# A cross-attention, state-space and feed-forward layer on one core: two carry schedules, a shared buffer across a phase boundary, and the last two blocks of the quantised feed-forward

## The reference, cut to what matters

```
c   = mean over heads of top-32 attention(x, ctx) @ V                # attention stage
x1  = layernorm(x)*(1 + film) + film                                  # modulate
y   = s4d(x1)                     # K = 2 Re sum_n C' exp(dt A l), causal convolution over 256 tokens
xt  = x + y*(1 + film) + film;  xt += gelu(layernorm(xt)@W1+b1)@W2+b2;  x2 = x + layernorm(xt)
# quantised feed-forward, on layernorm(x2)
xq  = round(x*127/max|x|) per token;  wq = ternary weights
h   = silu(depthwise_conv3(xq @ w1q) + b)
out = x2 + (round(h*127/max|h|) @ w2q) * (max|h|/127) * mean|w2|
```

## Time and profile before

| | us |
|---|---|
| three runs | 4005.41, 4005.66, 4013.56 |
| median | 4005.66 |
| profiled execution: its time | 4004.6 |
| its span | 4002.8 |
| busy in the span: PE, DVE, ACT, POOL | 3197.8, 2965.5, 2268.3, 1585.6 |
| s4d, by its first and last instructions | about 2027 to 2551 |
| feed_forward | about 2551 to 3547.9 |
| bit_feed_forward | 3547.9 to the end |

### The profile page before, as it was taken

The page is one execution under the profiler, slowest core; times in us unless marked ns, Lnnn a source line. Parts: engine busy times, 40 slices in busy tenths (PEclk is TensorE's granted clock), DMA queues, the critical chain, the costliest instruction groups (busy, mean ns, idle before and its releaser), DMA issues. The chain is left out here.

```text
span 4002.8 us, 54326 instructions
## 1 busy us (share of the span) xinstructions
PE 3197.8 (80%) x17201; PEld 2126.4 (53%) x17201; DVE 2965.5 (74%) x7375; ACT 2268.3 (57%) x2924; POOL 1585.6 (40%) x1268
## 2 busy tenths in 40 slices
PE   7547758887776787777977777589999999948998
PEld 3224334444443344445755555377777777736775
DVE  7789999999999999984569987434444443469897
ACT  4478779898985898971123333133323322337876
POOL 0025556555664555665300010013333232217775
PEclk9858878888887788878999998799999999979999
DMA  8700000000000000002213343633444443440212
GB/s 310 265 33 10 10 8 10 12 10 10 10 13 7 10 10 10 10 5 101 83 48 81 87 95 84 178 120 124 131 129 129 132 127 83 122 101 15 67 49 65
DMA packets 263201, 290.53 MB, mean 73 GB/s; under 512 B 53805, under 2 KB 176319, under 8 KB 261893
## 3 DMA queue, kind: packets, MB, share of 16 engines
q1 hardware_dynamic: 241112, 254.05, 21.2%
q10 hardware_dynamic: 18764, 18.34, 1.6%
q0 software_dynamic: 3040, 14.94, 1.0%
HBM read 218.82 MB, written 68.45 MB: 72 GB/s over the span
## 5 line engine op out<-in xcount | busy, mean ns | idle before, releaser
L1103 PE MATMUL up<-ctx,attnT 128*128 128x384 f32 (+1 forms) x1664 | 706.8, 580 | 45.0 <-ACT attnT L973 45.0
L1075 PE MATMUL score<-KT,q 64*128 64x512 f32 (+1 forms) x1792 | 385.5, 524 | 346.3 <-ACT S L933 243.5
L830 DVE MAX8 cand<-S 128x8 f32<-128x146 f32 (+1 forms) x2816 | 601.3, 295 | 53.7 <-ACT S L933 34.6
L789 POOL TENSOR_TENSOR S<-S 128x512 f32<-128x512 f32 (+1 forms) x224 | 424.7, 1929 | 354.9 <-DVE S L835 354.9
L1103 PEld LDWEIGHTS up<-ctx,attnT 128*128 128x128 f32 (+1 forms) x1664 | 361.6, 228 | 314.7 <-issue 149.8
L835 DVE SCALAR_TENSOR_TENSOR S<-S,tops,E 128x3202 f32<-128x3202 f32 x128 | 472.8, 3757 | 14.6 <-ACT E L964 14.6
L1075 PEld LDWEIGHTS score<-KT,q 64*128 64x128 f32 x1792 | 174.3, 237 | 547.2 <-ACT S L933 397.9
L933 ACT ACTIVATE S<-score 128x1024 f32<-128x1024 f32 (+1 forms) x448 | 402.9, 931 | 87.8 <-PE score L1075 87.0
L2179 DVE TENSOR_TENSOR ff_gelu<-ff_whole,ff_gelu 128x512 fp32r<-128x512 f32 x128 | 97.3, 761 | 427.2 <-ACT ff_gelu L2373 427.2
L942 ACT ACTIVATE E<-S,below 128x3202 bf16<-128x3202 f32 x128 | 379.6, 2966 | 40.3 <-DVE below L870 19.4
L964 ACT ACTIVATE E<-S,ebias 128x3202 f32<-128x3202 f32 x128 | 376.4, 2965 | 23.8 <-DVE S L835 13.4
(11 more groups left out here) (422 smaller groups left out, 5976.6 us busy)
## 6 DMA issues: line engine op xcount, KB each, us to landing
s_hankel<-scratch_K SPq DMA_DIRECT2D x128, 256.0 KB, 4.5
ff_w_low<-scratch_w1l SPq DMA_DIRECT2D x112, 256.0 KB, 2.7
ff_w_low<-scratch_w2l SPq DMA_DIRECT2D x112, 256.0 KB, 2.8
xt_prep<-in_x SPq DMA_DIRECT2D x8, 1024.0 KB, 8.7
scratch_xt<-xt_prep SPq DMA_DIRECT2D x8, 1024.0 KB, 8.2
next_prep<-in_ffn_w_t POOLq DMA_DIRECT2D x8, 1024.0 KB, 11.4
q<-scratch_qt SPq DMA_DIRECT2D x128, 64.0 KB, 1.9
mod_xt<-in_x_turned SPq DMA_DIRECT2D x32, 256.0 KB, 2.6
```

The source lines that it names most:

```text
L789: nc.gpsimd.tensor_tensor(S[:, b, 0, chunk(j)], S[:, b, 0, chunk(j)], S[:, b, 1, chunk(j)], ALU.add).then_inc(s["summed01"], 1)
L830: nc.vector.max(cand[:, h, 8 * k:8 * k + 8], S[:, b, h, k * SEG:min((k + 1) * SEG, G)])
L1075: last = nc.tensor.matmul(score[bank(p, j)][:, e, 0:w], lhsT=q[at, b, part, h // 2, :], rhs=KT[at, h // 2, chunk(j)], start=(part == 0), s ...
L1103: last = nc.tensor.matmul(up[:, 0:DV], lhsT=attnT[0:w, e, c - 4 * g, :], rhs=ctx[0:w, c, :], start=(c == 0), stop=(c == GC - 1))
```

## The change

In s4d a carry takes `first` (a part) and `halves` (one part or two). The first pair and the last pair are carried in two single steps of half the width; table(3) comes ahead of the first carry; `S_ready` counts parts. `chunk_turn(0)` comes ahead of `kernel_weights(1)` on POOL.

Between the feed-forwards: two tensors, `wide` and `lead`, outlive both. In feed_forward they hold y, u, q, qT, h and the film and bias rows; in bit_feed_forward `wide` holds the rounded hidden rows `gq`, `lead` the q and steps of a block and the ones. At the end of feed_forward SP loads block 0's q and steps into `lead` and two quarters of W1 into `wide`. The last group's stores count on a semaphore that is awaited in bit_feed_forward only (load(7), and the first writes to `gq`). The last steps are turned by PE into four rows of 128, copied by ACT and stored from there.

At the end of bit_feed_forward ACT rounds six j of block 7 and DVE two (`quantise_late`); PE takes blocks 7 and 8 piece by piece, j outside and k inside, each j when it is rounded, into eight different banks; block 8's x2 rows go to the free `conv` and are loaded ahead.

```diff
@@ s4d, POOL
-                        pool.wait_ge(s["S_ready"], G)
+                        pool.wait_ge(s["S_ready"], 2 * G)
-                for g in range(PARTS):
-                    if g:
-                        kernel_weights(g)
-                    if g % 2:
+                chunk_turn(0)
+                for g in range(1, PARTS):
+                    kernel_weights(g)
+                    if g % 2 and g > 1:
                         chunk_turn(g // 2)
@@ s4d, DVE
-                def carry(G):
+                def carry(first, halves):
...
+                    width = GP * halves
+                    at = slice(GP * (first % 2), GP * (first % 2) + width)
...
-                    dve.wait_ge(s["U_copied"], UG * 2 * (G + 1))
+                    dve.wait_ge(s["U_copied"], UG * (first + halves))
...
-                    add(2).then_inc(s["S_ready"], 1)
+                    add(2).then_inc(s["S_ready"], halves)
...
-                for G in range(PARTS // 2 - 1):
+                table(2)
+                table(3)
+                carry(0, 1)
+                carry(1, 1)
+                for G in range(1, PARTS // 2 - 1):
                     table(2 * G + 2)
-                    carry(G)
+                    carry(2 * G, 2)
                     table(2 * G + 3)
-                carry(PARTS // 2 - 1)
-                dve.wait_ge(s["S_ready"], PARTS // 2)
+                carry(PARTS - 2, 1)
+                carry(PARTS - 1, 1)
+                dve.wait_ge(s["S_ready"], PARTS)
@@ s4d, PE
-                    pe.wait_ge(s["S_ready"], g // 2 + 1)
+                    pe.wait_ge(s["S_ready"], g + 1)
@@ feed_forward, SP, ahead of store_x(QUADS - 1)
+                sp.wait_ge(s["qT_stored"], 16 * (QUADS + 1))
+                sp.wait_ge(s["rowstep_stored"], 16 * (QUADS + 1))
+                sp.wait_ge(s["modulated"], QUAD * QUADS)
+                sp.wait_ge(s["film_read"], QUAD * QUADS)
+                sp.wait_ge(s["biased"], QUADS)
+                lead_q, lead_step = lead_of(both)
+                sp.dma_start(lead_q, dram["qT"][:, :, MARGIN - 1:MARGIN + BIT_STEP + 1]).then_inc(passed_on["lead_in"], 16)
+                sp.dma_start(lead_step, dram["rowstep"][0:BIT_STEP + 2].partition_broadcast(P)).then_inc(passed_on["lead_in"], 16)
+                for k in range(2):
+                    sp.dma_start(early_w1_of(both, k), dram["w1q"][:, :, k * BANK:(k + 1) * BANK]).then_inc(passed_on[f"w1_in{k}"], 16)
@@ feed_forward, ACT
-                    if k == 0:
+                    if k == 0 and g < QUADS - 1:
...
+                act.wait_ge(s["rowstep_turned"], 1)
+                nc.scalar.activation(step_row, fp[0][0:QUAD, 0:P], ACT.Copy).then_inc(s["rowstep_row"], 1)
                 for k in range(QUAD):
                     copy_q(QUADS - 1, k)
-                act.wait_ge(s["qT_stored"], 16 * (QUADS + 3))
-                act.wait_ge(s["rowstep_stored"], 16 * (QUADS + 2))
+                act.wait_ge(s["rowstep_row"], 1)
+                act.dma_start(dram["rowstep"][QUAD * P * (QUADS - 1) + 1:QUAD * P * QUADS + 1].rearrange("(k p) -> k p", p=P), step_row).then_inc(passed_on["last_q_stored"], 16)
+                act.wait_ge(s["qT_stored"], 16 * (QUADS + 1))
+                act.wait_ge(s["rowstep_stored"], 16 * (QUADS + 1))
@@ feed_forward, PE
+                pe.wait_ge(s["gelu_done"], FC * QUADS)
+                pe.wait_ge(s["rowstep_ready"], QUADS)
+                nc.tensor.transpose(fp[0][0:QUAD, 0:P], rowstep[:, (QUADS - 1) % 2], const["ident"][:]).then_inc(s["rowstep_turned"], 1)
@@ bit_feed_forward
-    BY_ACT = [5] * (BLOCKS - 2) + [JC, 3]
+    BY_ACT = [5] * (BLOCKS - 2) + [6, 3]
...
+        gq = both["wide"][:].bitcast(BF16).rearrange("p (b f t) -> p b f t", b=2, f=FC)
...
-        out_at[BLOCKS - 2][2:] = hp[0][:, 0, :], hp[0][:, 1, :]
-        out_at[BLOCKS - 1][:2] = hp[1][:, 0, :], hp[1][:, 1, :]
+        out_at[BLOCKS - 2] = [hp[k // 2][:, k % 2, :] for k in range(QUAD)]
+        out_at[BLOCKS - 1] = [op[0], op[1], mp.rearrange("p k t -> p (k t)"), step_rows]
@@ bit_feed_forward, SP
-                load(0)
-                for k in range(HID // BANK):
+                sp.dma_start(taps[:], a["conv_w_cols"]).then_inc(s["taps_in"], 16)
+                sp.dma_start(tap_bias[:], a["conv_b_cols"]).then_inc(s["taps_in"], 16)
+                for k in range(2, HID // BANK):
...
+                    if m == BLOCKS:
+                        sp.wait_ge(s["raised"], ALL)
+                        for k in range(QUAD):
+                            sp.dma_start(last_x2[0:rows(BLOCKS - 1), k], dram["x2"][rows_at(BLOCKS - 1, k), :]).then_inc(s["last_x_in"], 16)
@@ bit_feed_forward, POOL
                     pool.wait_ge(s["scaled"], JC * n + j + 1)
+                    if n == 0 and j == BY_ACT[n]:
+                        pool.wait_ge(passed_on["last_q_stored"], LAST_Q)
@@ bit_feed_forward, DVE
+                def quantise_late(n):
+                    dve.wait_ge(passed_on["last_q_stored"], LAST_Q)
+                    for j in range(BY_ACT[n], JC):
+                        dve.wait_ge(s["scaled"], JC * n + j + 1)
+                        v.tensor_scalar(gq[:, n % 2, 2 * j:2 * j + 2, 0:QUAD * rows(n)], part(n, j), ROUND, ROUND, ALU.add, ALU.subtract).then_inc(s["late_quantised"], 1)
...
+                    if i == ALL + STEPS_AT - JC:
+                        quantise_late(BLOCKS - 2)
                     if i == ALL - JC + SCALE_AT:
                         quantise_last(BLOCKS - 1)
@@ bit_feed_forward, PE
+                def pieces(n, order, begin, end):
+                    r = rows(n)
+                    for j in order:
+                        if j < BY_ACT[n]:
+                            pe.wait_ge(s["rounded"], by_act(n) + j + 1)
+                        else:
+                            pe.wait_ge(s["late_quantised"], by_pool(n) - by_pool(BLOCKS - 2) + j - BY_ACT[n] + 1)
+                        for k in range(QUAD):
+                            for f in (2 * j, 2 * j + 1):
+                                last = nc.tensor.matmul(out_at[n][k][0:r, :], lhsT=gq[:, n % 2, f, r * k:r * (k + 1)], rhs=W2q[:, f, :],
+                                                        start=(j == begin and f == 2 * j), stop=(j == end and f == 2 * j + 1))
...
+                pe.wait_ge(s["tapped"], ALL)
+                pieces(BLOCKS - 2, range(3), 0, JC - 1)
+                turn_top(BLOCKS - 1)
+                pieces(BLOCKS - 2, range(3, 4), 0, JC - 1)
+                spread_steps(BLOCKS - 1)
+                pieces(BLOCKS - 2, range(4, JC), 0, JC - 1)
+                pe.wait_ge(s["y_ready"], QUAD * (BLOCKS - 2))
+                pe.wait_ge(s["scale_ready"], BLOCKS)
+                pieces(BLOCKS - 1, (3, 0, 1, 4, 2, 5, 6, 7), 3, 7)
```

More of the change, by code:

```diff
@@ L1609, in carry @@
                     for k in range(1, BLOCKS):
-                        v.tensor_tensor(r, blocks[:, :, k - 1, BLOCK - 1, :].unsqueeze(2).broadcast_to([P, 2, 2, BOTH]), turn[:, BLOCK - 1], ALU.mult)
+                        v.tensor_tensor(r, blocks[:, :, k - 1, BLOCK - 1, :].unsqueeze(2).broadcast_to([P, 2, 2, width]), turn[:, BLOCK - 1, :, :, at], ALU.mult)
                         dve.drain()
@@ L1823, with lead_of, early_w1_of, feed_forward @@
 LEVEL = 127.0
-def feed_forward(nc, sem, const, a, mean, dram):
+BIT_ROWS = 114
+BIT_STEP = QUAD * BIT_ROWS
+def lead_of(both):
+    lead = both["lead"]
+    qin = lead[:, 0:DC * (BIT_STEP + 2) // 2].bitcast(BF16).rearrange("p (c t) -> p c t", c=DC)
+    return qin, lead[:, DC * (BIT_STEP + 2) // 2:DC * (BIT_STEP + 2) // 2 + BIT_STEP + 2]
+def early_w1_of(both, k):
+    return both["wide"][:, DC * BANK // 2 * k:DC * BANK // 2 * (k + 1)].bitcast(BF16).rearrange("p (c f) -> p c f", c=DC)
+def feed_forward(nc, sem, const, a, mean, dram, both, passed_on):
     scope, sb, ps = phase_scope(nc)
@@ L2575, in _, with bit_feed_forward @@
                     turn(g)
+                pe.wait_ge(s["gelu_done"], FC * QUADS)
+                pe.wait_ge(s["rowstep_ready"], QUADS)
+                nc.tensor.transpose(fp[0][0:QUAD, 0:P], rowstep[:, (QUADS - 1) % 2], const["ident"][:]).then_inc(s["rowstep_turned"], 1)
                 for k in range(QUAD):
                     turn_q(QUADS - 1, k)
-def bit_feed_forward(nc, sem, const, a, mean, dram, out):
+def bit_feed_forward(nc, sem, const, a, mean, dram, out, both, passed_on):
     scope, sb, ps = phase_scope(nc)
@@ L2595, in bit_feed_forward @@
         W2q = sb("bf_W2q", [P, FC, D], BF16)
-        rowstep = sb("bf_rowstep", [P, STEP + 2])
+        qin, rowstep = lead_of(both)
         taps = sb("bf_taps", [P, FC, 3])
@@ L2611, in bit_feed_forward @@
         diag = sb("bf_diag", [P, STEP])
-        every = sb("bf_every", [P, P])
+        every = both["lead"][:, 3 * D - P:3 * D]
         scale = sb("bf_scale", [P, 2, STEP])
@@ L2743, in _ @@
                         scaling(n, j)
-                    for j in range(BY_ACT[n], JC):
```

(29 more changed lines are left out.)

93 lines of the change are left out of this document (47 added, 46 removed).

## The result

The changed kernel takes 3964.86 us, the median of four runs (3963.56 to 3965.55), against 4005.53 for the kernel before in the same comparison (four runs, 4003.22 to 4013.56): a ratio of 0.9895, 95% interval 0.9877 to 0.9912. The profiled execution took 3965.5, with a span of 3963.7. The forecast was 3964, and "faster".

The account below looks back on a forecast made before the run. DVE was taken to pace s4d, with PE waiting at its end and 20 us without computing at the barrier. Terms -8.1 - 9.0 - 14.9 - 9.1 = -41.1 from 4004.6 give 3963.5, with the median's 1.1 about 3964; range 3955 to 3977.

Parts of the forecast that it names:

- Front: Start of s4d: table(3) fills DVE's 17.2 us wait for ACT's states, first pair carried in halves; -8.1 us.
- The half carry of 16.0 us: s4d: a whole carry of 22.9 us less 6.9 for half-width instructions; two halves take 32.0, 9.1 more than one whole.
- End: End of s4d: PE's 12.1 us wait goes, 1.9 more from spread(14), 5 lost to the store before Hankel loads; -9.0 us.
- the 1.9 us at the lower clock: End of s4d: without the pause spread(14) takes 11.8 us instead of 13.7, whose first matmuls ran at the lower clock.
- the sum would be 5 us lower without ring order: End of s4d: loads stand behind the whole output store on SP's queue; without that rule the sum would be 5 us lower.
- Barrier: Between the feed-forwards: ACT no longer waits for its last stores, and DVE's product starts at once on early-loaded data; -14.9 us.
- hidden: Barrier: transposing the steps on PE and copying on ACT fall in idle time; uncovered they would cost 1 us.
- Tail: Last blocks of bit_feed_forward: PE works in pieces, the end set by block 7's last x2 load; -9.1 us.
- the one in which loads bound the last spreads: Rival, end of s4d: Hankel loads make spreads 14 and 15 take 16.5 and 15 us, giving 3969; chance 0.10.
- The rival with the low clock in the middle of the quantised layer: Rival "slower": PE granted 1.2 GHz for some blocks, each about 40 us longer; two blocks give 4044; chance 0.03.
- The low clock in the tail: Rival: PE stays at the lower clock through all tail pieces, 3.54 us each, giving 3990; chance 0.07.

Follow-up runs that it names:

- y_by_act: Changed kernel, with the output store between spread(13) and spread(14) issued by ACT on its own queue instead of by SP: 3967.67 us.
- both_moved: Changed kernel, with that output store on ACT's queue and block 7's last x2 load issued ahead of block 7's first output store: 3967.15 us, ratio 0.9902.
- s4d_only: The kernel before the change, with only the function s4d taken from the changed kernel: 3990.90 us.

## Why the prediction was right

- **Front, -8.1 forecast, -7.0 measured** (8.0 at table(4), counted from the first cut). The half carry of 16.0 us was right (16.4 and 16.0), and the wait of 17.2 us went. About 1.0 of the gain was lost on the long way to gather(15). The working counted the halves as a cost of 9.1 us; against the wait for the ring slot that a whole carry brings they cost nothing.
- **End, -9.0 forecast, -9.3 measured.** PE's wait of 12.1 us for the carry went, and spread(14) came at 16.9 where 16.8 was forecast (11.8 and 5). That this size was right is in part luck. The 5.3 us over spread(15)'s 11.65 are 3.5 of longer waits for loads (4.8 against 1.3) and some 1.8 of the lower clock: the 1.9 us at the lower clock that the working took away came back behind the new stall. The sentence that the sum would be 5 us lower without ring order is not borne out. With the loads out of that order PE waited less for them, by 0.2 us in y_by_act and by 2.9 in both_moved, but longer stretches at the lower clock took it back, and stage B is 59.5 and 58.7 us. From the end of spread(13) to that of spread(15) it was 37.6 us before and is 28.6 now, 9.0 less.
- **Barrier, -14.9 forecast, -14.7 measured** (-13.6 against s4d_only). DVE's product came 2.5 us behind ACT's last store of rows (2.3 forecast). The two that the prediction names, the missing wait and the early loads, are enough: with unturned steps and no wait the stage is 2.1 us. The transposition, which it called "hidden", costs 0.4 us there. Turned steps would have taken 6.1 us out by themselves had the wait stayed.
- **Tail, -9.1 forecast, -9.0 measured** (E and F together). By its own steps: from turn_top to DVE's first scaling 4.8 us (4.7 forecast), five scalings and roundings 13.9 (13.9), the wait for the last load ending 6.9 behind the first finish (6.9), then 3.4 (3.5). The last finish ends 29.0 us behind turn_top, as forecast. What it left out is that the last stores land 1.5 us later when they come bunched. That was made up by luck: turn_top came 1.9 us late against PE's end of the block before (2.2 forecast), and the blocks ahead of the tail were 1.1 shorter.
- **The other terms.** feed_forward got 0.7 longer, in a stage that varies by as much. Of the rivals, the one in which loads bound the last spreads had spread(14) right (16.5), but not spread(15) (15, where it took 11.65). The rival with the low clock in the middle of the quantised layer did not come: the clock there is 1.00, with PE busy 42.3 of 45 us. The low clock in the tail did not either: 32 matmuls took 7.07 us.
- **The sum.** The span of the profiled execution got 39.1 us shorter, 2.0 less than the 41.1 of the working: 1.1 of it at the front and 0.7 in feed_forward. The medians lie 40.7 apart. That the median came within 1 us of the forecast (3963.5 and 1.1 give 3964.6, which the working rounds to 3964) is closer than its terms were, and the changed kernel timed again gave 3967.19.

## What to carry to other kernels

When an engine waits for a producer, look for work of its own that is ready and put it ahead of the wait; splitting the step behind the wait pays only where a consumer is waiting for its first half. When a stall behind a store is made shorter by issuing the store on another queue or in pieces, look at PE's busy time too: here up to 2.9 us of waits went, and as much came back as matmuls at the lower clock. Scattered stores of a few bytes per packet cost those behind them, not themselves. Either take away the wait for that queue or turn them; once one is done, the other gives this stage nothing or little. And cut the stages of two traces at the same events before you compare totals.

## What was not expected of the hardware

- 512 packets of 4 bytes, each booked with 8 ns, made the packets of 512 bytes behind them on the queue take up to 2.4 us each in the mean of a microsecond (28 ns where the steps were turned), and the last store land 10.5 us after its issue instead of about 2. The Trainium skill, "DMA: Bandwidth & Descriptors", Specifications, says that transfers under 512 bytes make the DMA engine read, modify and write. That fits, but no run here shows the mechanism, and the store of parts 12 and 13, with packets of 256 bytes, ran at 20 ns a packet.
- Shorter waits of PE for loads did not make two spreads shorter: the granted clock was 0.80 and 1.00 in them with 6.0 us of such waits, and 0.70 and 0.84 with 3.2.
- One execution ran with PE four to five times slower throughout, and its trace has no record of the clock. A granted clock of 1.00 can mean that none was recorded.
